# Reordering an in-order pipeline: the gray image two iterations ahead, the mask product first, and a reordered drain

## The reference, cut to what matters

```python
h = edges(gray(x))                       # 16 images of 256x256; Scharr filter, sum of absolute values / 2
h = concat(h, embed(x_txt))              # 16 sequences of 384 rows (256 image rows, 128 text rows) x 256
h = h + attention(layernorm(h))          # 16 heads of 16, each row sees itself and the 128 rows before it
n = layernorm(h); h = h + where(top288(n @ w_router), gelu(n @ w_block), n)
h = h + state_space(layernorm(h))        # a linear recurrence over the 384 rows, plus D * u
n = layernorm(h)
h = h + shared_mlp(n) + sum over the 2 best of 8 experts of gate * expert_mlp(n)
```

## Time and profile before

| | |
|---|---|
| median of three runs | 2193.65 us (2190.08 to 2194.74) |
| the profiled execution, its time | 2192.07 us |
| its span, first to last instruction | 2190.3 us |
| PE busy | 1965.9 us (90% of the span), mean granted clock 0.969 of full |
| PEld, DVE busy | 1559.6 us (71%), 1350.6 us (62%) |
| ACT, POOL busy | 1079.5 us (49%), 819.2 us (37%) |

### The profile page before, as it was taken

How to read it: one execution, slowest core, us unless ns; L and a number is a source line. 1 busy time by engine, 2 the same in 40 slices (tenths; PEclk the granted TensorE clock), 3 DMA queues, 4 the chain that set the end, 5 groups by cost and what they waited for, 6 DMA issues and landing times.

```text
span 2190.3 us, 44925 instructions
## 1 busy us (share of the span) xinstructions
PE 1965.9 (90%) x13651; PEld 1559.6 (71%) x13652; DVE 1350.6 (62%) x3572; ACT 1079.5 (49%) x2513; POOL 819.2 (37%) x1535
## 2 busy tenths in 40 slices
PE   2879999999999999999999999985789999999997
PEld 1546666666666666666666666653689999999997
DVE  5647668577576685775766757643455565555654
ACT  0336455455554554555545555541355455555553
POOL 3113324334243233342432333322344545454454
PEclk8789999999999999999999999996899999999998
DMA  4220211211202112112021121110333232323322
GB/s 138 65 58 9 66 45 29 65 35 45 65 15 65 44 28 65 33 47 65 15 65 43 30 65 31 35 59 8 111 84 84 44 83 47 81 48 81 48 47 40
DMA packets 81090, 116.53 MB, mean 53 GB/s; under 512 B 20965, under 2 KB 61509, under 8 KB 78725
## 3 DMA queue, kind: packets, MB, share of 16 engines
q1 hardware_dynamic: 54948, 85.34, 14.1%
q0 software_dynamic: 23360, 27.91, 7.8%
q10 hardware_dynamic: 2736, 2.76, 0.4%
HBM read 51.58 MB, written 26.71 MB: 36 GB/s over the span
## 4 chain that ended last, share of the span: by engine, by line
PE 51%; DVE 16%; issue 14%; POOL 8%; DMA 5%; ACT 4%; POOLq 0%; DVEq 0%; SPq 0%; ACTq 0%
PE ps L1780 10%; PE ps L1616 8%; POOL slot_rows L658 4%; PE ps L1493 4%; PE ps L1792 3%; PE ps L1791 3%; PE ps L1793 3%; DVE mx L1119 2%; PE ps L1582 2%; PE ps L1465 2%; DMA result<-yb,idx_o 2%; PE ps L1607 2%; PE ps L1561 2%; PE ps L1548 2%; DMA slot_rows<-pay,row_i 2%
## 5 line engine op out<-in xcount | busy, mean ns | idle before, releaser
L793 ACT ACTIVATE prob<-ps,mx 128x256 f32<-128x256 f32 (+1 forms) x768 | 295.0, 443 | 254.9 <-DVE mx L1119 240.1
L897 ACT ACTIVATE hid_hi<-ps,b 128x256 fp32r<-128x256 f32 x408 | 205.8, 504 | 286.1 <-PE ps L1780 286.1
L1119 DVE TENSOR_REDUCE mx<-ps 128x2 f32<-128x512 f32 (+1 forms) x384 | 224.5, 594 | 116.0 <-PE ps L1540 107.3
L785 ACT ACTIVATE pT<-ps 128x512 f32<-128x512 f32 (+1 forms) x384 | 205.2, 534 | 123.9 <-PE ps L1548 120.5
L1395 DVE TENSOR_TENSOR hid_lo<-hid_full,hid_hi 128x256 fp32r<-128x256 f32 x408 | 172.3, 426 | 150.7 <-ACT hid_full L900 150.1
L1539 PE MATMUL ps<-ks,qs 96*128 96x512 f32 (+1 forms) x384 | 186.7, 487 | 63.9 <-ACT prob L793 51.0
L1791 PE MATMUL ps<-w_hi,hid_hi 128*128 128x256 f32 x816 | 232.3, 285 | 0.0
L1792 PE MATMUL ps<-w_lo,hid_hi 128*128 128x256 f32 x816 | 227.9, 279 | 0.0
L1793 PE MATMUL ps<-w_hi,hid_lo 128*128 128x256 f32 x816 | 227.9, 279 | 0.0
L900 ACT ACTIVATE hid_full<-ps,b 128x256 f32<-128x256 f32 x408 | 206.2, 505 | 0.0
L1548 PE MATMUL ps<-ident,prob 128*128 128x128 f32 x1280 | 204.8, 277 | 0.0
(11 more groups left out here) (269 smaller groups left out, 4175.6 us busy)
## 6 DMA issues: line engine op xcount, KB each, us to landing
w_raw<-in_w SPq DMA_DIRECT2D x16, 1024.0 KB, 6.0
xin<-in_x SPq DMA_DIRECT2D x32, 384.0 KB, 3.6
qs<-q_hi SPq DMA_DIRECT2D x128, 96.0 KB, 2.1
ks<-k_hi SPq DMA_DIRECT2D x256, 48.0 KB, 2.1
qs<-q_lo SPq DMA_DIRECT2D x64, 96.0 KB, 2.1
ks<-k_lo SPq DMA_DIRECT2D x128, 48.0 KB, 2.1
xn_rows<-xc SPq DMA_DIRECT2D x16, 384.0 KB, 2.5
result<-h SPq DMA_DIRECT2D x16, 384.0 KB, 2.5
```

The lines of the kernel that those rows point to most:

```text
L785: act.activation(pT[:, u % TB, :, k0:2, :], ps[:, 2 + u % 2, :].rearrange("p (h k q) -> p h k q", h=2, k=2)[:, :, k0:2, :], ACT.Copy).then ...
L793: ins = act.activation(prob[:, s % PB, hh, w], ps[:, s % 2, hh * 2 * P + w.start:(hh + 1) * 2 * P], ACT.Exp, bias=mx[:, s % 2, hh:hh + 1])
L897: act.activation(hid_hi[:, f], ps[:, f % 4, 0:CHUNK], ACT.Gelu_apprx_tanh, bias=b1[half][:, f:f + 1])
L1119: dve.tensor_reduce(mx[:, s % 2], sc, AX_X, ALU.max, negate=True).then_inc(max_done.sem, 1)
```

## The change

The names and numbers are those of the diff; "ahead" is a new flag of the sequences on SP and DVE.

1. **Gray image.** The five operations of `make_gray` no longer stand in slot 11 for sequence `b + 1`. They stand in slots 24 (two), 26 (two) and 27 (one) for sequence `b + 2`. SP loads the image of `b + 2` behind `store_h4(b - 2)` and copies its halo behind `stack(b + 1)`.
2. **Mask product first.** In each attention unit the bf16 product with the mask starts the accumulation and the product of queries and keys ends it.
3. **Maxima first.** In slots 14, 20 and 21 (`LATER`) DVE does its attention unit ahead of the chain's piece; the statistics of the third layernorm move from slot 20 to 21.
4. **PE's order.** The queries' projection goes ahead of the unit of slot 26. The product with `wo` goes ahead of the products with the values. The first third of `values_sum` goes behind the unit of slot 1. The first turn of the chain waits for the seventh hidden block only, and for the eighth ahead of its second half. (`drive` is a function now, in the same place.)
5. **Drain.** In iteration 16 POOL's dispatch of sequence 14 goes behind `states`. The ranks of sequence 15, and ACT's exponential for them, go into slot 30, ahead of seven of the eight hidden blocks. `shared_sum` of sequence 15 goes between the fourth and the fifth copy into `flat`. PE waits for it ahead of its first turn of an expert's rows.
6. **Experts.** POOL gathers chunk `j + 2` before it waits for the landing of the rows added for chunk `j - 1`.

```diff
-TEXT, GRAY_AT, TURN1 = 3, 11, 12
+TEXT, TURN1 = 3, 12
+GRAYS = {24: (0, 1), 26: (2, 3), 27: (4,)}
+LATER = (STATE, OUT + 1, OUT + 2)
...
-            def sequence(b, late, chain, head):
-                if head:
-                    load_image(b + 1)
+            def sequence(b, late, chain, head, ahead):
                 if late:
                     store_h4(b - 2)
-                if head:
-                    load_halo(b + 1)
+                if ahead:
+                    load_image(b + 2)
                 if chain:
                     store_rows(b - 1)
                 if head:
                     stack(b + 1)
+                if ahead:
+                    load_halo(b + 2)
...
             def sequence(b, att, late, chain, head):
-                if late:
+                if late and att:
                     dispatch(b - 2)
                 if chain:
                     chain_deviations(b - 1, 1)
                     direct_term(b - 1)
                     states(b - 1)
+                if late and not att:
+                    dispatch(b - 2)
...
                             yb[:, k], None, compute_op=ALU.add).then_inc(y_stored.sem, 16)
-                pool.wait_ge(y_stored.sem, y_stored.at(j, 32))
-                pool.sem_inc(y_sent.sem, 1)
...
+            def rows_added(j):
+                pool.wait_ge(y_stored.sem, y_stored.at(j, 0))
+                pool.sem_inc(y_sent.sem, 1)
...
                 with pool.Fori(lo, hi) as j:
                     gather_rows(j, 2)
+                    rows_added(j)
                     add_rows(j)
...
+                    if first_weights and s == min(UPS):
+                        gate_ratio(b - 1)
...
                                       ).then_inc(h3_ready.sem, 1)
                     dve.wait_ge(h3_ready.sem, h3_ready.at(b, 1))
+                if s == OUT + 2:
                     chain_rows(b, 2)
...
-                    if chained:
+                    if chained and s not in LATER:
                         chain(b - 1, s)
                     if att and s == 2:
                         values_sum(b)
                     if att:
                         unit(b, s)
+                    if chained and s in LATER:
+                        chain(b - 1, s)
...
-                    if head and s == GRAY_AT:
-                        make_gray(b + 1)
+                    if first and s == TURN1 - 1:
+                        for n in range(5):
+                            make_gray(b + 1, n)
+                    for n in GRAYS.get(s, ()) if ahead else ():
+                        make_gray(b + 2, n)
...
-            shared_sum(NB - 1)
             dve.wait_ge(route_loaded.sem, route_loaded.at(0, 16))
             for e in range(NE):
...
+                if e == 3:
+                    shared_sum(NB - 1)
...
-                    pe.matmul(dst, qs[:, r, m, i * P:(i + 1) * P], ks[:, r, :, m, keys], start=True, stop=False)
-                    pe.matmul(dst, ident_bf[:], mask_bf[:, :, c0:2 * P], start=False, stop=True
+                    pe.matmul(dst, ident_bf[:], mask_bf[:, :, c0:2 * P], start=True, stop=False)
+                    pe.matmul(dst, qs[:, r, m, i * P:(i + 1) * P], ks[:, r, :, m, keys], start=False, stop=True
                               ).then_inc(scores_done.sem, 1)
...
+                if n == 0 and not first:
+                    pe.wait_ge(hid_ready.sem, hid_ready.at(b - 1, FB - 1))
                 pe.wait_ge(xc_ready.sem, xc_ready.at(b, n + 1))
                 pe.wait_ge(xcT_ready.sem, xcT_ready.at(b, n))
-                if n == 0:
-                    pe.wait_ge(hid_ready.sem, hid_ready.at(b, 0))
...
                 for k in range(KB):
+                    if n == 0 and k == 1:
+                        pe.wait_ge(hid_ready.sem, hid_ready.at(b, 0))
...
+                    if head and s == TURN2 - 1:
+                        queries(b + 1)
                     if att and s == BLOCK:
-                        values_sum(b)
+                        values_sum(b, 1, NT)
...
                     if att:
                         unit(b, s)
+                    if att and s == TURN0:
+                        values_sum(b, 0, 1)
...
-                    if head and s == TURN2 - 1:
-                        queries(b + 1)
...
+                    if last and s == min(UPS):
+                        slot_ranks(b - 1, False)
...
+            pe.wait_ge(h4_ready.sem, h4_ready.at(NB, 0))
             turn_chunk(0)
```

More of the change, by code:

```diff
@@ L523, in _ @@
             stack(0)
[L524 to L528 removed]
+            load_image(1)
+            load_halo(1)
+            sequence(0, False, False, True, True)
+            sequence(1, False, True, True, True)
+            with sp.Fori(2, NB - 2) as b:
+                sequence(b, True, True, True, True)
+            sequence(NB - 2, True, True, True, False)
+            sequence(NB - 1, True, True, False, False)
             def load_weights(e):
@@ L1066, in make_rows @@
             def make_rows(b):
+                head_step.steps = 0
                 dve.wait_ge(abs_done.sem, abs_done.at(b, 2))
@@ L1298, in split_first, with sequence @@
                     dve.tensor_tensor(w1_lo[0][:], w1_raw[:], w1_hi[0][:], ALU.subtract)
-            def sequence(b, att, late, chained, head, first=False, first_weights=False):
+            def sequence(b, att, late, chained, head, ahead, first=False, first_weights=False):
                 att_step.steps = 0
@@ L1337, in sequence @@
                     chain_scale(b, 0)
-            make_gray(0)
+            for n in range(5):
+                make_gray(0, n)
             make_text(0)
@@ L1517, in values, with values_sum @@
                 ins.then_inc(proj_done.sem, 1)
-            def values_sum(b):
+            def values_sum(b, first, last):
                 pe.wait_ge(v_ready.sem, v_ready.at(b, 1))
                 pe.wait_ge(h1_ready.sem, h1_ready.at(b, 0))
-                for i in range(NT):
+                for i in range(first, last):
                     ins = pe.matmul(ps[:, 5, D:2 * D].rearrange("p (h d) -> p h d", h=NH), ones9[:], vaug[:, i, :, 0:DK],
                                     start=(i == 0), stop=(i == NT - 1))
-                ins.then_inc(sumv_done.sem, 1)
+                if last == NT:
+                    ins.then_inc(sumv_done.sem, 1)
             def unit(b, s):
@@ L1687, in logits, with sequence @@
                     ins.then_inc(logit_done.sem, 1)
-            def sequence(b, att, late, chained, head, first=False):
+            def sequence(b, att, late, chained, head, first=False, last=False):
                 for s in range(SLOTS):
-                    if first and s == 1:
+                    if first and not chained and s == 1:
                         pe.wait_ge(mats_read.sem, mats_read.at(0, 1))
@@ L1746, in _ @@
             pe.wait_ge(late_loaded.sem, late_loaded.at(0, NLATE))
-            sequence(1, True, False, True, True)
+            sequence(1, True, False, True, True, first=True)
             with pe.Fori(2, NB - 1) as b:
@@ L1750, in _ @@
             sequence(NB - 1, True, True, True, False)
-            sequence(NB, False, True, True, False)
-            slot_ranks(NB - 1, False)
+            sequence(NB, False, True, True, False, last=True)
             for n in range(2 * NT):
```

84 lines of the change are left out of this document (44 added, 40 removed).

## The result

The changed kernel takes 2130.32 us (median of 4 runs, 2123.96 to 2133.31) against 2192.05 for the kernel before in the same batch: ratio 0.9714, interval 0.9686 to 0.9742. Forecast was 2129.0 in 2105 to 2169, with 0.92 on faster. The profiled execution took 2132.92 us, span 2131.1, 59.2 less than the 2190.3 of before.

What follows compares the result with a forecast made beforehand. PE was taken to bound the loop, with late local hand-overs. Loop 41, iterations 0 and 15 2, drain 13 and experts 9 make 65 us off 2192.07: 2127, so a median of 2129, range 2105 to 2169.

Steps and rivals of the forecast that it cites:

- Gray image: Loop, slot 11: moving it removes PE's waits of 1.09 and 0.24 us; gain 1.1 us, bounds 0.5 and 1.33.
- rival C: Loop: the gray image in its new place holds up the keys, making the kernel slower, 2240 us; chance 0.05.
- Slots 20 to 26: Loop: three PE gaps, 2.43 us, shrink while `xn` comes later; gain 0.75 us an iteration, bounds 0 and 2.43.
- Mask product: Attention units: the shorter weight load is the one left unhidden; gain 0.6 us an iteration, bounds -2.2 and +2.2.
- Rival D: Attention units: the heavier weight load isn't hidden, each unit costs 0.09 us more; 2167 us, chance 0.06.
- Slots 0 to 2: Loop start: earlier first turn and a third of `values_sum` fill two PE gaps; gain 0.5 us, bounds 0 and 1.07.
- Iterations 0, 1 and 15: Loop ends: iteration 1 gains the full 2.9 us, iterations 0 and 15 part of it, 2 us together.
- Dispatch of 14: Drain, POOL: root starts 3.6 us earlier, dispatch overruns its new hole by about 0.6; gain 3.0 us, bounds 0 and 3.6.
- Ranks of 15: Drain: counting in slot 30 brings the first expert product 10.0 us earlier, 9.7 after ACT's table switch; bounds 7 and 11.
- Experts: Expert phase: gathers no longer wait for added rows to land; gain 9 of PE's 10.0 us of waits, bounds 2 and 10.
- Rival A: Loop: all gaps close because DVE keeps up in slots 20 to 22; 2092 us, chance 0.12.
- B: Loop gives nothing as gaps return as other waits; only drain and experts' 22 us stay, 2171 us; chance 0.17.

Runs made afterwards that it cites:

- the ranks experiment: Changed kernel with PE's count of sequence 15's experts and ACT's gate ratio back behind the hidden blocks, shared sum still between the copies: 2136.18 us, ratio 0.9753.
- the last dispatch experiment: Changed kernel with LATER empty, third statistics back in slot 20, and the drain's dispatch of sequence 14 behind the third root: 2095.44 us, ratio 0.9562.
- the first experiment: Changed kernel with LATER empty: chain pieces ahead of the maxima in slots 14, 20 and 21, third statistics back in slot 20; 2102.72 us, ratio 0.9594.

## Why the prediction was right, and where only its sum was

The kernel got faster for the reasons given, but the total met the median within 1.3 us partly by luck. The loop's 13 periods gave 5 us less than forecast and the other iterations 4.4 less; the experts gave 4.5 more. For the profiled execution the sum said 2127, and it took 2132.92, 5.9 more. The prediction then put the median 1.6 us above that execution; it came out 2.6 us below, and that closed most of the distance.

*Gray image.* Right in kind: both waits went, the cover held, rival C had nothing behind it. The size was off: 1.8 us where 1.1 was taken and 1.33 was the upper bound. PE's busy time fell by another 0.4 with the waits, which the bound, made of gaps alone, left out; why it fell isn't shown. The 2.9 us of DVE work, against the 4 taken, agree with the reading that the copy's 1.92 us came from POOL's work beside it: the copy now takes 0.43 at 898.52, when POOL has no work (its last operation, for `hb`, ends at 897.73). The Trainium skill ("SBUF — State Buffer", on the shared port pair) has the pair held by DVE or GpSimd for a whole instruction, and the trace agrees. What stands beside `hb` now is the scaling of `xc`, and it takes 2.26 us where it took 1.05 before.

*Slots 20 to 26.* Forecast 0.75, of three gaps less what `xn` costs. PE's order there was worth 2.05 in this kernel, the maxima ahead in slots 20 and 21 minus 0.94: 1.1 together, the clock included (without it 1.65 - 0.41 - 0.39 = 0.85, close to the forecast). The step that failed is the first of its sentences: "the maximum of unit 20 in front removes the first" gap was booked as a gain of 1.06, with `xn` 0.8 us late and nearly paid for. In fact the turn of `xn` waits 1.85 us and PE, in order, can do nothing meanwhile, so the edit of slots 20 and 21 alone is a loss. In slot 14, whose cost the prediction put at 0.25, it is 0.62. The sum also had no term for the clock, which falls behind that wait in some iterations.

*Mask product.* Forecast 0.6, measured 0.38 between iterations at full clock; the 0.54 between the means includes a fall of the clock more. The rule of the Trainium skill ("TensorE: Matmul & The Clock Gate", on LDWEIGHTS pulled ahead) that the prediction weighed would have made the order worth nothing; the two windows, PE busy 81.53 against 82.06, don't bear that out for these short products. Rival D is refuted.

*Slots 0 to 2.* Forecast 0.5. The two gaps of 0.42 and 0.65 are 0.19 and 0.23 now, which is 0.65. These two edits weren't undone alone. Between iterations at full clock the single effects of the other parts are 1.75 (gray image), 0.38 (mask), 1.65 (PE's order) and -1.47 (maxima), 2.3 together, against 87.82 - 85.18 = 2.64 for all. That leaves 0.3 for slots 0 to 2, if the parts add.

*Iterations 0, 1 and 15.* Forecast 2 and 2.9, measured 1.3 - 0.8. The 1.3 lies well within what the stretch up to iteration 1 varies by (218.4 to 227.8 us), so it shows nothing. In iteration 15 PE is busy 68.40 us against 69.32 before, but idle 9.77 against 8.04: the maxima ahead cost more waiting there than the rest saved.

*Dispatch of 14.* Forecast 3.0, measured 0. The mis-sized term is the overrun, "by about 0.6". It is 1470.76 - 1467.2 = 3.6 us, for two reasons: the first of the six issues takes 2.87 us, not 1, beside DVE's split of weights (1459.06 to 1462.13), so that dispatch and landing take 10.6 us and not 8.5; and the statistics come 7 us behind `states`, not 8.2, since the state space's products on PE between them took 4.5 us here against 5.3 in the execution read before, more of which lay at the lower clock.

*Ranks of 15.* Forecast 9.7, measured 7.1. The mechanism was right; what is late next is `shared_sum`, as the prediction said, but DVE waits 3.50 us for the down products there, and the last four copies and the split come behind them, 4.32 us of PE. The rest of the drain's gain, 5.2 us, was in no step. Part of it is the move of `shared_sum` itself. Before, the store of its result was issued ahead of the gather, and the gather took 1555.97 - 1548.38 = 7.6 us to land. With `shared_sum` between the copies, ranks still behind, it took 1517.41 - 1513.16 = 4.25. The timelines of before (POOL's issue and PE's turn) and of the ranks experiment (POOL's issue; the turn is shown above):

```profile
1548.38 1.02 POOL L701 DMA_INDIRECT xg<-xn_rows,idx_s  x1 [0.85 <-POOL idx_s L697]
...
1555.97 1.08 PE L1764 MATMUL ps<-ident,xg 128*128 128x128 f32 x4 [14.05 <-DMA xg<-xn_rows,idx_s]
```

```profile
1513.16 1.02 POOL L709 DMA_INDIRECT xg<-xn_rows,idx_s  x1 [0.85 <-POOL idx_s L705]
```

That is 3.3 of the 5.2 us. That the store is what delayed the gather is argued from this order, not shown by a run of its own. The remaining 1.9 us are no more than the drain varies by without an edit in it: with the gray image alone it took 110.06 us instead of 111.87.

*Experts.* Forecast 9 with 10 as the upper bound, measured 12.6 to 13.5. Mis-sized was the wait's price: it is its length plus what the clock loses behind it, some 2.5 us behind the longest. The bound was made of the 10.0 us of waits alone.

Rival A (2092) was nearest in spirit: with the maxima put back, the loop gains 4.1 us an iteration of the 5.4 it had, and with the dispatch moved too, 2095 is reached, some 6 us of it by the experts' stretch, whose cause is open (below). B fell with the period.

## What to carry to other kernels

An edit that removes a wait has to be tried alone. Here the parts together won 62 us, and one of them, which did remove its 1.06 us wait, lost 24. On a full in-order engine, moving one consumer's work forward moves another's back, and the order with the smaller listed wait isn't the faster one unless the new waiter has other work. A long job that waits for its landing belongs in the stretch where its queue has nothing due; put into one that is 3.6 us too short, it returned what it gained. And a mean over iterations mixes the edit with whatever the clock did: the lengths of the single iterations, with the granted clock of each, tell the two apart.

## What the runs showed that was not expected

A wait costs PE more than its length. Behind the wait of 1.85 us (at `xn`) and towards the end of the one of 6 us (at the gather) the granted clock fell to 0.50. But it did not fall at every such wait: behind the 1.85 us it did in one iteration of 13 in the changed kernel, in three with the ranks moved, although the loop is the same, and in eight with PE's old order. In iteration 15, behind a wait of 2.3 us, it fell in the last dispatch experiment (76.26 us) and not in the first experiment (74.57), with the same code. No run here settles what decides it. A fall cost 0.8 to 1.5 us net in the loop, as much as many of the edits.

The experts' code is the same in most of these kernels, and PE hardly waits in it, yet the stretch from the first expert product to the end took 617 to 618 us in five profiled executions (2131.1 - 1512.97 = 618.1 for the changed kernel) and 611.8 to 612.8 in six (first experiment, 2100.2 - 1487.45 = 612.75). The groups of PE show where: one of the second layer's three kinds of products, first of the changed kernel, then of the first experiment (busy us, mean ns):

```profile
L1829 PE MATMUL ps<-w_lo,hid_hi 128*128 128x256 f32 x816 | 227.5, 279 | 0.0
```

```profile
L1828 PE MATMUL ps<-w_lo,hid_hi 128*128 128x256 f32 x815 | 225.2, 276 | 0.0
```

The kernel before ran at 279 as well, so its comparison with the changed one isn't touched; a comparison of the changed kernel with the first or last experiment has some 5 us from this. Its cause stays open. The time up to iteration 1 also varies, from 218.4 to 227.8 us, between kernels that do the same there. That is why each verdict above rests on a period or a stretch, with the clock beside it, and the medians only confirm it.
